# Turning listed rows: from two TensorE transpositions to one VectorE transposition of 32x32 blocks, with the rows loaded by blocks

## The chip, the cores and the metric

The kernel runs on one core of a Trainium2 chip. The metric is the device time of one execution in microseconds (us), lower is better. Three runs of the kernel before gave 1203.69, 1200.79 and 1199.48 us, median 1200.79.

The engines are TensorE (PE; PEld is its weight load), VectorE (DVE), ScalarE (ACT), GpSimd (POOL) and SyncE (SP), which issues most DMAs. "SPq" in a row is SyncE's own instruction queue.

## The reference

Two layers, each a residual block: x = x + ffn(cond(x)). x holds 64 samples of 64 channels by 1024 elements, so 4096 rows of 1024, float32.

```python
# layer 0
c0 = grouped_conv1d(x, L0_cond_weight, taps=9, groups=4) + (cond_128 @ L0_cond_c_weight.T)[:, :, None] + bias
base = c0 @ base_w.T + base_b
hidden = c0 @ A.T                              # 64 ranks
w, e = top2(softmax(c0 @ router_w.T))          # 2 of 16 experts, weights divided by their sum
x = x + base + 0.5 * sum_k(w_k * hidden @ B[e_k].T)
# layer 1
att = softmax(mlp(cond_128))                   # 8 mixtures
c1 = (sum_m att_m * weight_m) @ x + sum_m att_m * bias_m     # a 64x64 mixing of the channels, per sample
g = top2 of 28 gates (c1 @ gate_W.T), softmax over the two
x = x + c1 @ base_W.T + lora_up(2 * g * (c1 @ lora_A.T))     # 28 experts of rank 8
```

The change is in `w_k * hidden @ B[e_k].T` of layer 0: each row goes through two of sixteen matrices of 64 by 1024.

## The kernel before

**Tiles.** The 4096 rows are 32 tiles of 128. `step0` handles a tile of layer 0, `step1` one of layer 1; every engine has its own program with functions of these names, and they meet at semaphores. In a step TensorE multiplies the turned tile (`yh`, `yl`, high and low part) by the weights in three banks: `z[2]` holds the small columns (with the 64 ranks and the gates), `z[0]` and `z[1]` the rest. All products are made of three float32r matmuls (high x high, low x high, high x low), as `three` writes them.

**Lists.** Rather than multiplying each row by all sixteen `B`, the kernel sorts. In `step0` VectorE scales the row's 64 ranks by its two weights (`listed`), and GpSimd scatters the two copies (`scatter`) into `hs_dram`, where every expert has a list of its own. When a wave of 16 tiles is through, TensorE multiplies the lists by the experts' matrices, a listed tile of 128 rows at a time. Four listed tiles (`PER`) make a listed step, twelve listed steps (`WS`) a wave. Wave 0 is worked off beside the tiles 18 to 29 of layer 0, wave 1 beside the tiles 2 to 13 of layer 1. The products go to `zs_dram`, and GpSimd adds them to the rows with gathering DMAs in layer 1.

**A listed step before the change.** SyncE loads four tiles of 128 rows by 64 ranks (`load_ht`), each as 128 rows of 256 B, two side by side in one buffer `ht[j]` of 128x128; a register read from the table `tab_row` says which tile. It also loads the experts' matrices `bd` (`load_bd`, which waits until TensorE is done with the last ones) and stores the products (`store_zs`). TensorE turns the two buffers with two transpositions into the PSUM bank `prep` (`turn_ht`, line 1508), so that ranks lie on the partitions: two experts' 64 ranks in 128. ScalarE copies the bank as the high part `hh` (`ht_high`), VectorE subtracts it for the low part `hl` (`ht_low`), and one step later TensorE multiplies: `listed_pair(s, 0)` after the small bank, `listed_pair(s, 1)` after `z[0]` in layer 0 and after `z[1]` in layer 1. ScalarE copies the products out (`outputs`, tiles `zt`).

**Where the turning stands.** TensorE has it in `step0` behind `rank` and ahead of the conv of the tile after next (line 1670), and in `step1` ahead of the last matmuls `over_h` (line 1747). VectorE has `ht_low` at the end of `step0`, behind `rank0`, and in `step1` ahead of the two adds that empty `z[0]` and `z[1]` (line 1433). SyncE has the loads for listed step s + 1 at the start of `listed_step`, ahead of the `bd` loads. The order on each engine is that of the written code; there is no scheduler.

**SyncE and the output adds.** In `step1` SyncE loads the rows of the tile after next but one (`load_xr`) and starts `listed_step` only when VectorE has emptied both banks of the tile before.

## Time and profile before

| | |
|---|---|
| median of 3 runs | 1200.79 us |
| the profiled execution, its own time | 1200.46 us |
| its span | 1198.5 us |
| PE busy | 1171.6 us, 98% |
| ACT busy | 767.6 us, 64% |
| DVE busy | 706.4 us, 59% |
| POOL busy | 297.5 us, 25% |
| DMA | 267.15 MB, mean 223 GB/s |
| mean granted TensorE clock | 0.998 |

The profile is of one execution. Times count from the start of the span. A busy time is that in which at least one instruction of the engine ran; idle time of an engine that isn't the bottleneck costs nothing. The lists of wave 0 are worked off from about 302 to 530 us, those of wave 1 from about 600 to 868 us.

### The profile page before, as it was taken

How to read it: one execution, taken by the hardware profiler on the slowest of the kernel's cores; microseconds unless marked ns; L12 is line 12 of the kernel's file. 1: busy time of each engine (PE TensorE's matmuls, PEld its weight loads, DVE VectorE, ACT ScalarE, POOL GpSimd, SP SyncE). 2: the span in 40 equal slices, each digit the busy share in tenths (PEclk: the TensorE clock that was granted, in tenths of full speed). 3: DMA queues.
4: the chain of work that ended last, by engine and by line, in shares of the span. 5: the costliest groups of instructions: out<-in, count | busy, mean ns of one | idle time of the engine just before them, and what ended most of it. 6: DMA issues, size and time to landing. Idle time of an engine off the chain costs nothing.

```text
span 1198.5 us, 22055 instructions
## 1 busy us (share of the span) xinstructions
PE 1171.6 (98%) x6783; PEld 1034.3 (86%) x6783; DVE 706.4 (59%) x1985; ACT 767.6 (64%) x1746; POOL 297.5 (25%) x315
## 2 busy tenths in 40 slices
PE   6999999999999999999999999999999999999998
PEld 6999999999899999898787787787788888888887
DVE  6677778777465655557764444454445555555552
ACT  5566667666586776864667767767645665755751
POOL 4111733323222223234312112111131222222200
PEclk9999999999999999999999999999999999999999
DMA  9566566775999999979699999999875455455410
GB/s 333 185 241 258 191 225 229 285 268 165 253 319 327 311 322 311 325 269 242 127 245 304 268 293 311 281 292 299 269 165 118 99 123 110 118 123 118 110 53 36
DMA packets 84698, 267.15 MB, mean 223 GB/s; under 512 B 23248, under 2 KB 27472, under 8 KB 77360
## 3 DMA queue, kind: packets, MB, share of 16 engines
q1 hardware_dynamic: 72608, 230.12, 58.4%
q0 software_dynamic: 11600, 36.06, 17.0%
q8 instruction: 24, 0.39, 0.1%
q10 hardware_dynamic: 432, 0.30, 0.1%
q14 instruction: 34, 0.28, 0.1%
HBM read 154.24 MB, written 112.20 MB: 222 GB/s over the span
## 4 chain that ended last, share of the span: by engine, by line
PE 41%; DMA 7%; SPq 1%; issue 1%; DVE 1%; ACT 1%; POOL 0%; ACTq 0%; POOLq 0%; DVEq 0%
PE z L1461 12%; PE z L1462 12%; PE z L1463 12%; DMA ht<-hs_dram 3%; DMA xin<-zs_dram,gpos 2%; DMA xin<-x_dram 1%; PE c L1461 1%; PE c L1463 1%; PE c L1462 1%; PE c L1528 1%; PE prep L1725 1%; DMA x<-zs_dram,gpos 1%; DVE xb L1433 1%; PE c L1532 1%; PE c L1530 1%
## 5 line engine op out<-in xcount | busy, mean ns | idle before, releaser
L754 ACT ACTIVATE moved<-mid 32x256 f32<-32x256 f32 x944 | 392.2, 415 | 139.0 <-DVE mid L1023 114.6
L1461 PE MATMUL z<-w_1h,yh 128*128 128x384 f32 (+1 forms) x512 | 190.0, 371 | 0.0
L1461 PE MATMUL z<-w_0h,yh 128*128 128x384 f32 (+1 forms) x512 | 187.4, 366 | 0.2 <-DVE xb L1433 0.2
L1463 PE MATMUL z<-w_1l,yh 128*128 128x384 f32 (+1 forms) x512 | 185.8, 363 | 0.0
L1463 PE MATMUL z<-w_0l,yh 128*128 128x384 f32 (+1 forms) x512 | 185.8, 363 | 0.0
L1462 PE MATMUL z<-w_1h,yl 128*128 128x512 f32 (+1 forms) x504 | 183.0, 363 | 0.0
L1462 PE MATMUL z<-w_0h,yl 128*128 128x512 f32 (+1 forms) x504 | 182.8, 363 | 0.0
L669 POOL TENSOR_TENSOR carrier<-ones_col 128x1 f32<-128x1 f32 x96 | 25.5, 266 | 539.1 <-DVE den L1117 131.8
L1461 PE MATMUL z<-w_2h,yh 128*128 128x336 f32 (+1 forms) x512 | 152.9, 299 | 2.1 <-DVE yl L1031 2.1
L1463 PE MATMUL z<-w_2l,yh 128*128 128x336 f32 (+1 forms) x512 | 152.5, 298 | 0.0
L1462 PE MATMUL z<-w_2h,yl 128*128 128x252 f32 (+1 forms) x504 | 149.9, 297 | 0.0
L661 POOL TENSOR_TENSOR xb<-xin,bias0b 128x1024 f32<-128x1024 f32 x32 | 78.3, 2447 | 246.0 <-DMA x_dram<-xb 232.5
L812 ACT ACTIVATE e<-top,negm 128x2 f32<-128x2 f32 x64 | 18.4, 287 | 169.4 <-DVE negm L1058 169.4
L1044 DVE STREAM_TRANSPOSE mid<-moved 128x512 f32<-128x512 f32 x58 | 37.9, 691 | 134.2 <-ACT moved L754 134.2
L1461 PEld LDWEIGHTS z<-w_0h,yh 128*128 128x128 f32 x512 | 96.1, 188 | 15.0 <-issue 4.4
L1031 DVE TENSOR_TENSOR yl<-mid,yh 128x512 fp32r<-128x512 f32 x116 | 74.8, 685 | 57.8 <-PE z L1463 57.8
L1461 PEld LDWEIGHTS z<-w_1h,yh 128*128 128x128 f32 x512 | 96.2, 188 | 13.6 <-issue 4.4
L1463 PEld LDWEIGHTS z<-w_1l,yh 128*128 128x128 f32 x512 | 96.1, 188 | 10.4
L1463 PEld LDWEIGHTS z<-w_0l,yh 128*128 128x128 f32 x512 | 96.1, 188 | 10.2
L1462 PEld LDWEIGHTS z<-w_0h,yl 128*128 128x128 f32 x504 | 94.6, 188 | 10.2
L1462 PEld LDWEIGHTS z<-w_1h,yl 128*128 128x128 f32 x504 | 94.7, 188 | 9.2
L1461 PEld LDWEIGHTS z<-w_2h,yh 128*128 128x128 f32 x512 | 96.5, 188 | 4.0 <-issue 2.6
(217 smaller groups left out, 2587.8 us busy)
## 6 DMA issues: line engine op xcount, KB each, us to landing
bd<-bd_dram SPq DMA_DIRECT2D x96, 512.0 KB, 9.0
zs_dram<-zt SPq DMA_DIRECT2D x96, 512.0 KB, 10.2
hs_dram<-zt SPq DMA_DIRECT2D x34, 512.0 KB, 6.6
x8raw<-in_x_dram SPq DMA_DIRECT2D x32, 516.0 KB, 4.4
xin<-in_x_dram SPq DMA_DIRECT2D x32, 512.0 KB, 6.9
x_dram<-xb SPq DMA_DIRECT2D x32, 512.0 KB, 5.2
out_dram<-xb SPq DMA_DIRECT2D x32, 512.0 KB, 4.7
bd_dram<-bd SPq DMA_DIRECT2D x8, 1024.0 KB, 6.5
```

The costliest lines, as they stand in the source:

```text
L661: nc.gpsimd.tensor_tensor(xb[u][:, :], xin[u][:, :], bias0b[:, :], ALU.add).then_inc(xb_ready, 1)
L669: nc.gpsimd.tensor_tensor(carrier[:, :], ones_col[:, :], ones_col[:, :], ALU.add).then_inc(carried, 1)
L754: return nc.scalar.activation(o, i_, ACT.Copy)
L812: nc.scalar.activation(e12[:, :], top8[:, 0:2], ACT.Exp, bias=negm[:, :], accum_out=e12sum[:, :]).then_inc(s.exp, 1)
L1031: V.tensor_tensor(o, v, turned_rows(s, t, yh[u], b)[0], ALU.subtract).then_inc(s.y_lo[b], 1)
L1044: mm = V.transpose(mid[:, :].rearrange("p (k q r) -> p q k r", k=KC, r=Q)[:, :, k, :], moved[:, :].rearrange("p (q k c) -> p q k c", k=KC, ...
L1433: V.tensor_tensor(xb[u][:, w], z[b][:, 0:w.stop - w.start], x1[v][:, w], ALU.add)\
L1461: T.matmul(o, ah, wh, start=start, stop=False, **kw)
L1462: T.matmul(o, al, wh, start=False, stop=False, **kw)
L1463: return T.matmul(o, ah, wl, start=False, stop=stop, **kw)
L1528: T.matmul(o[half][:, :], hh[ranks(v), j, :], bd[j][ranks(v), 0, w], start=True, stop=False)
L1530: T.matmul(o[half][:, :], hl[ranks(v), j, :], bd[j][ranks(v), 0, w], start=False, stop=False)
```

## The change

Where a buffer `ht[j]` held 128 rows by 128 columns, the new `ht` holds 32x32 blocks. SyncE loads each listed tile in two DMAs instead of one, one for each half of its 64 columns. A DMA fills 32 partitions: the 128 rows are four blocks of 32, which lie side by side, and each run is 32 columns, 128 B. A block so lies in the quadrant (the group of 32 partitions) in which its columns have to stand after turning. One VectorE transposition, which turns every 32x32 block in its place, then makes the whole `ht_turned` for the four tiles. TensorE's `turn_ht` goes; ScalarE and VectorE read `ht_turned` instead of the bank. The semaphore `ht_ps` becomes `ht_done`, raised by VectorE; SyncE waits for it before it reloads `ht`. The four waits for the loads (`ht_in`) stand on VectorE now.

```diff
--- before.py
+++ after.py
@@ -172,7 +172,8 @@
         braw = [sb(over, f"braw{w}", [2 * R0, L]) for w in range(2)]
         over.close()
         bd.append(sb(ctx, "bd1", [2 * R0, 2, L], F32R))
-        ht = [sb(ctx, f"ht{j}", [P, 2 * R0]) for j in range(PER // 2)]
+        ht = sb(ctx, "ht", [P, PER // 2, P // Q, Q])
+        ht_turned = sb(ctx, "ht_turned", [2 * R0, PER // 2, P])
         hh = sb(ctx, "hh", [2 * R0, PER // 2, P], F32R)
         hl = sb(ctx, "hl", [2 * R0, PER // 2, P], F32R)
         mbrow = sb(ctx, "mbrow", [P, 1])
@@ -331,8 +332,8 @@
         ht_in = [sem(f"ht_in{v}") for v in range(4)]
         bd_in = [sem(f"bd_in{v}") for v in range(4)]
         zs_out = [sem(f"zs_out{v}") for v in range(4)]
-        ht_ps, hh_ready, hl_ready, zt_ps, zt_out = (
-            sem(n) for n in ("ht_ps", "hh_ready", "hl_ready", "zt_ps", "zt_out"))
+        ht_done, hh_ready, hl_ready, zt_ps, zt_out = (
+            sem(n) for n in ("ht_done", "hh_ready", "hl_ready", "zt_ps", "zt_out"))
         x1_hi, x1_lo = sem("x1_hi"), sem("x1_lo")
         mbrow_ready = sem("mbrow_ready")
         mprod_done, msum_done, mix_hi, mix_lo, mix_zero = (sem(n) for n in ("mprod_done", "msum_done", "mix_hi", "mix_lo", "mix_zero"))
@@ -343,7 +344,7 @@
 
         x_t = x.rearrange("s c l -> (s c) l").rearrange("(t p) l -> t p l", p=P)
         out_t = out.rearrange("s c l -> (s c) l").rearrange("(t p) l -> t p l", p=P)
-        hs_t = [a.rearrange("(t p) c -> t p c", p=P) for a in hs_dram]
+        hs_q = [a.rearrange("(t q p) c -> t p q c", p=Q, q=P // Q) for a in hs_dram]
         zs_t = [a.rearrange("(t p) c -> t p c", p=P) for a in zs_dram]
         x1_t = x1_dram.rearrange("(t p) l -> t p l", p=P)
         hs_parts = [a.rearrange("(p j r) c -> j p (r c)", p=P, c=R0, r=L // R0) for a in hs_dram]
@@ -443,10 +444,12 @@
 
             def load_ht(s, w, first=False):
                 if not first:
-                    sp.wait_ge(ht_ps, s)
+                    sp.wait_ge(ht_done, s)
                 for v in range(PER):
                     at = sp.value_load(tab_row[0:1, PER * s + v, :], min_val=0, max_val=E0 * CAP // P - 1)
-                    sp.dma_start(ht[v // 2][:, ranks(v)], hs_t[w][at]).then_inc(ht_in[v], 16)
+                    for i in range(R0 // Q):
+                        p = R0 * (v % 2) + Q * i
+                        sp.dma_start(ht[p:p + Q, v // 2, :, :], hs_q[w][at, :, :, Q * i:Q * (i + 1)]).then_inc(ht_in[v], 16)
 
             def load_bd(s, v, first=False):
                 e = sp.value_load(tab_expert[0:1, PER * s + v, :], min_val=0, max_val=E0 - 1)
@@ -825,11 +828,11 @@
 
             def ht_high(s, first=False):
 
-                act.wait_ge(ht_ps, s + 1)
+                act.wait_ge(ht_done, s + 1)
                 if not first:
                     act.wait_ge(zt_ps, PER * s)
                     act.wait_ge(hl_ready, s)
-                copy(hh[:, :, :].rearrange("p j r -> p (j r)"), prepp[:, 0:PER // 2 * P]).then_inc(hh_ready, 1)
+                copy(hh[:, :, :], ht_turned[:, :, :]).then_inc(hh_ready, 1)
 
             def outputs(s, v, banks, first=False):
 
@@ -1209,10 +1212,14 @@
                 mix_sum(t)
                 mix_low(t)
 
+            def ht_turn(s):
+                for v in range(PER):
+                    dve.wait_ge(ht_in[v], 16 * R0 // Q * (s + 1))
+                V.transpose(ht_turned[:, :, :].rearrange("p j (q r) -> p j q r", r=Q), ht[:, :, :, :]).then_inc(ht_done, 1)
+
             def ht_low(s):
                 dve.wait_ge(hh_ready, s + 1)
-                V.tensor_tensor(hl[:, :, :].rearrange("p j r -> p (j r)"), prepp[:, 0:PER // 2 * P],
-                                hh[:, :, :].rearrange("p j r -> p (j r)"), ALU.subtract).then_inc(hl_ready, 1)
+                V.tensor_tensor(hl[:, :, :], ht_turned[:, :, :], hh[:, :, :], ALU.subtract).then_inc(hl_ready, 1)
 
             step = [0]
 
@@ -1315,6 +1322,8 @@
                 residual(i, u, 1)
                 if tables:
                     tiles_of_lists(0)
+                if turn is not None:
+                    ht_turn(turn)
                 rank0(t, u, w)
                 if turn is not None:
                     ht_low(turn)
@@ -1422,6 +1431,7 @@
                 if at(t, 0):
                     tiles_of_lists(1)
                 if turn is not None:
+                    ht_turn(turn)
                     ht_low(turn)
 
                 dve.wait_ge(x1_stored[u], 16 * (TILES // 2))
@@ -1504,18 +1514,6 @@
                         mm = T.transpose(tp[n][:, P * g:P * (g + 1)], mid[:, NB * (GROUPS * n + g):NB * (GROUPS * n + g + 1)],
                                          ident[:, :])
                     mm.then_inc(a0.y_ps[n], 1)
-
-            def turn_ht(s, first=False):
-
-                for v in range(PER):
-                    pe.wait_ge(ht_in[v], 16 * s + 16)
-                if first:
-                    pe.wait_ge(tab_ready, 2)
-                else:
-                    pe.wait_ge(hl_ready, s)
-                for j in range(PER // 2):
-                    mm = T.transpose(prepp[:, P * j:P * (j + 1)], ht[j][:, :], ident[:, :])
-                mm.then_inc(ht_ps, 1)
 
             def listed_pair(s, j):
 
@@ -1666,8 +1664,6 @@
                     if first:
                         turn_conv(1)
                     rank(t, w)
-                if turn is not None:
-                    turn_ht(turn, first=at(turn, 0))
                 if exists(t + 2):
                     if lists:
                         pe.wait_ge(zt_out, PER * s + 3)
@@ -1743,8 +1739,6 @@
                 pe.wait_ge(a1.hT_lo, t + 1)
                 if first:
                     first_tiles(1)
-                if turn is not None:
-                    turn_ht(turn)
                 if first:
                     pe.wait_ge(lb_lo, 2)
                 for b in range(2):
```

TensorE in a step of layer 0 in wave 0, before (`z` and `c` are banks, `prep` the turned rows, `small_upper` and `small_ones` belong to the ranking):

```order
L1599 MATMUL z<-onehot,small_upper 128x32 [waits l0_z_out2,listed_ready]
L1600 MATMUL z<-before,small_ones 128x32
L1517 MATMUL prep<-ident,ht 128x128 [waits ht_in3,ht_in2,hl_ready,ht_in1,ht_in0]
L1517 MATMUL prep<-ident,ht 128x128
L1461 MATMUL c<-x8h,th 128x256 [waits x8_lo,l0_c_out0,x8_hi,zt_out]
```

and the same place now:

```order
L1473 MATMUL z<-w_1l,yh 128x384
L1597 MATMUL z<-onehot,small_upper 128x32 [waits l0_z_out2,listed_ready]
L1598 MATMUL z<-before,small_ones 128x32
L1471 MATMUL c<-x8h,th 128x256 [waits x8_lo,l0_c_out0,x8_hi,zt_out]
L1472 MATMUL c<-x8h,tl 128x256
```

The conv follows the ranking at once, and no instruction of TensorE waits for `ht_in`.

VectorE at the end of the same step now (`yl` is the low part of the next tile, `xb` the residual rows, `mid` the conv's output):

```order
L1034 TENSOR_TENSOR yl<-mid,yh 128x512 [waits l0_y_hi1]
L1282 TENSOR_TENSOR xb<-z,xb 128x384 [waits base_done1]
L1218 STREAM_TRANSPOSE ht_turned<-ht 128x256 [waits ht_in2,ht_in3,ht_in1,ht_in0]
L1113 TENSOR_REDUCE rank<-comb 128x2 [waits before_ready]
L1114 TENSOR_SCALAR placef<-idxf 128x2
L1116 TENSOR_TENSOR placef<-placef,rank 128x2 [waits before_ready]
L1118 CAST place_of<-placef 128x2 [waits before_ready]
L1120 COPY den<-placef 128x1
L1222 TENSOR_TENSOR hl<-ht_turned,hh 128x256 [waits hh_ready]
L1026 TENSOR_TENSOR mid<-c,cbT 128x2x2x128 [waits l0_c_ps0]
```

Before, the transposition was not there and `hl` read `prep`; the rest stood in the same order. The ranks, `hl` and the conv's output now stand behind the wait for the four loads.

SyncE's loads of one listed tile, before:

```order
L448 TENSOR_LOAD tab_row
L448 ISA x2
L449 ISA
L449 DMA ht<-hs_dram 128x64
L448 ISA
```

and now:

```order
L449 TENSOR_LOAD tab_row
L449 ISA x2
L452 ISA
L452 DMA ht<-hs_dram 32x4x32
L452 ISA
L452 DMA ht<-hs_dram 32x4x32
L449 ISA
```

One DMA and one register instruction are added for each tile, four of each in a listed step; the table is read as often as before.

## Rows read from the trace of the kernel before

**Rows 1.** The page, busy time, share of the span and instructions.
```profile
PE 1171.6 (98%) x6783; PEld 1034.3 (86%) x6783; DVE 706.4 (59%) x1985; ACT 767.6 (64%) x1746; POOL 297.5 (25%) x315
```

**Rows 2.** By stretch: busy times, then PEclk, DMA share, GB/s.
```profile
330.00:492.00 162.00, 162.00 (x1061) 147.45 (x1058) 97.80 (x294) 120.31 (x280) 40.00 (x33) 1.00 1.02 317
622.00:860.00 238.00, 235.43 (x1275) 188.40 (x1272) 111.92 (x295) 167.03 (x379) 44.88 (x52) 1.00 1.03 292
299.00:302.00 3.00, 0.11 (x3) 0.02 (x2) 2.49 (x10) 0.00 (x0) 0.19 (x1) 1.00 0.13 29
302.00:305.00 3.00, 2.98 (x16) 3.00 (x17) 0.57 (x2) 0.38 (x1) 1.96 (x2) 0.59 0.81 201
305.00:308.00 3.00, 3.00 (x21) 3.00 (x20) 1.23 (x2) 0.40 (x1) 0.00 (x0) 0.84 1.06 247
```

**Rows 3.** TensorE's waits: us in total, times, longest.
```profile
PE prep L1517 <- DMA ht<-hs_dram: 5.5, 5, 2.9
```

**Rows 4.** Timeline of TensorE, wave 0, with and without a turning: start, us.
```profile
341.18 0.18 PE L1600 MATMUL z<-before,small_ones 128*128 128x32 bf16 x1
...
341.37 0.36 PE L1461 MATMUL c<-x8h,th 128*128 128x256 f32 x1
...
529.82 0.18 PE L1600 MATMUL z<-before,small_ones 128*128 128x32 bf16 x1
529.85 0.36 PE L1461 MATMUL c<-x8h,th 128*128 128x256 f32 x1
```

**Rows 5.** The same in wave 1, with and without a turning.
```profile
621.86 0.39 PE L1532 MATMUL t<-bd,hh 64*128 64x512 f32 x1
...
622.37 0.48 PE L1461 MATMUL z<-lbh,h1h 112*128 112x512 f32 x1
...
864.86 0.39 PE L1532 MATMUL t<-bd,hh 64*128 64x512 f32 x1
865.18 0.50 PE L1461 MATMUL z<-lbh,h1h 112*128 112x512 f32 x1
```

**Rows 6.** Wave 0's start: SyncE's and TensorE's timeline; `bd` loads of 300:307.
```profile
296.81 3.63 SPq L449 DMA_DIRECT2D ht<-hs_dram  x4
301.20 4.76 SPq L455 DMA_DIRECT2D bd<-bd_dram  x4
...
310.43 0.49 PE L1528 MATMUL c<-bd,hh 64*128 64x512 f32 x1
...
L455 SPq DMA_DIRECT2D bd<-bd_dram x4: 487/504/553, 301.2 to 305.5; - x4
...
DMA to landing us min/median/max: 5.0/6.3/7.8
```

**Rows 7.** A step of wave 0: `ht` loads of 346:359, VectorE's timeline.
```profile
L449 SPq DMA_DIRECT2D ht<-hs_dram x4: 332/333/337, 346.7 to 350.3; - x4
...
DMA to landing us min/median/max: 7.6/8.9/10.2
...
361.70 0.55 DVE L1275 TENSOR_TENSOR xb<-z,xb 128x384 f32<-128x384 f32 x1
```

**Rows 8.** A late step of wave 1: `ht` loads of 672:688, VectorE's timeline.
```profile
L449 SPq DMA_DIRECT2D ht<-hs_dram x4: 337/338/363, 672.6 to 676.4; - x4
...
DMA to landing us min/median/max: 12.9/14.3/15.8
...
692.81 0.69 DVE L1433 TENSOR_TENSOR xb<-z,xin 128x512 f32<-128x512 f32 x1 [0.61 <-PE z L1463]
```

**Rows 9.** SyncE's waits from 322 to 492 us.
```profile
SPq L421 <- PE c L1463: 21.2, 9, 2.8
```

**Rows 10.** Durations min/median/max of DVE's transpositions; a wait; `hh`, `hl`.
```profile
L1040 DVE STREAM_TRANSPOSE mid<-moved x36: 400/402/446, 336.5 to 488.6; 128x256 f32<-128x256 f32 x36
...
DVE comb L1102 <- PE z L1600: 8.5, 9, 2.1
...
690.31 0.42 ACT L754 ACTIVATE hh<-prep 128x256 fp32r<-128x256 f32 x1
690.76 0.42 DVE L1214 TENSOR_TENSOR hl<-prep,hh 128x256 fp32r<-128x256 f32 x1 [1.07 <-ACT hh L754]
```

## The prediction

> **What bounds the kernel now.** I read the page first, for the engine that has no idle time. TensorE is busy for 1171.6 of 1198.5 us, all others for under two thirds of the span [rows 1]. So a microsecond counts if TensorE spends it or waits for it. Next, the rows by stretch: in the two stretches that work on lists (330 to 492 us and 622 to 860 us) TensorE is busy for 162.00 of 162.00 and 235.43 of 238.00 us, and the DMA share there is 1.02 and 1.03 [rows 2]. The reader should keep both: TensorE sets the pace there, and the DMA engines have nothing to spare that this view could show. Then TensorE's waits: for `ht`, the tile that the change touches, it waits 5 times, 5.5 us in all, the longest 2.9 us [rows 3]. That longest is the first step of wave 0, the other four are in wave 1 and sum to 2.6 us. Right behind the first one the granted clock is 0.59 for 3 us and 0.84 for the next 3 [rows 2]; at half speed part of that time, TensorE loses 3 x 0.41 + 3 x 0.16 = 1.7 us more than the wait itself.
>
> **What goes from TensorE.** 24 steps turn a listed group with two transpositions each. A single one is 272 to 331 ns long in the trace, but they overlap their neighbours, so what counts is start to start. In wave 0 the conv matmul starts 341.37 - 341.18 = 0.19 us after the ranking matmul where the pair stands between them, and 529.85 - 529.82 = 0.03 us where it doesn't [rows 4]: 0.16 us, twelve times, 1.9 us. In wave 1 it is 622.37 - 621.86 = 0.51 against 865.18 - 864.86 = 0.32 [rows 5]: 0.19 us, twelve times, 2.3 us. Together 4.2 us. The Trainium skill, VectorE: DVE Perf Modes, "The three transpose paths", lists 390 ns for a TensorE transposition of 128x128 and advises TensorE for it if PSUM will do as destination; at that price 48 of them would be 18.7 us, but the trace shows a quarter of it, because the pair is hidden in the pipeline, so by these rows the rule's advice costs little and its removal brings little.
>
> The four short waits of wave 1 go as well: 2.6 us [rows 3]. Nothing behind the missing transposition on TensorE needs `ht` directly; it needs `hl`, in its next step. What takes its place on VectorE is judged below.
>
> **The first step of wave 0.** Here the removed wait uncovers another. SyncE issues four `ht` loads from 296.81 to 300.44, and then four `bd` loads from 301.20 to 305.96 [rows 6]. A pair of `bd` halves is needed by the first listed pair on TensorE, which now starts at 310.43 [rows 6]. The second `bd` load is issued about 1.4 us after the first, at 302.6, and lands some 6 us later (the four take 5.0 to 7.8 [rows 6]), near 308.6. Without the 2.9 us wait, the 1.7 us of slow clock and the pair itself TensorE would be there at 305.6 and stand until `bd` lands. And `bd` lands later than before, because four more `ht` DMAs are issued ahead of it.
>
> What does one more DMA cost on SyncE? One that takes no new table entry: the instruction is 0.333 us [rows 7], with some register work around it; the full pitch of today's with the entry read from the table is (3.63 - 0.33) / 3 = 1.10 us [rows 6]. The bounds per step are 4 x 0.33 = 1.3 and 4 x 1.10 = 4.4 us. I take 0.5 each, 2.0 us, nearer to the bare instruction since the entry isn't read again. A DMA with more dimensions may be dearer: `bd`'s instruction is 0.504 us [rows 6]; with that for all eight it is 2.0 + 8 x 0.17 = 3.4 us.
>
> So `bd` lands near 310.6, TensorE stands for 5 us in place of 2.9, and goes on 0.2 us later than before. The clock then probably falls again as it did after the 2.9 us, which costs up to 1.7 us, of which I take 1.3. The term is a loss of 1.5 us. Its ends: if the landing did not move, a gain of 1.9 us; at 4.4 us for the issues a loss of 2.6 + 1.7 = 4.3 us.
>
> **What comes onto VectorE.** One transposition of 128x256 per step: the same form takes 0.402 us in the trace [rows 10]. In wave 0 it waits for `ht` after the third residual add, ahead of the ranks. In the step shown the last load is issued at 350.3 and lands 7.6 us later, at 357.9; VectorE ends that add at 361.70 + 0.55 = 362.25 [rows 7]. So 2 us of later landing fit, with 2.4 to spare. Behind it are queued the ranks (their scatter is GpSimd's, which idles), `hl`, and the conv output of the next tile, on which ScalarE's moves and the next transposition hang. That ring has some air: VectorE idles 8.5 us in 9 steps for the ranking matmul alone [rows 10], 0.9 us a step, against 0.4 added. ScalarE takes `hh` from SBUF instead of PSUM while it would wait for the conv output. Cost nothing; if the cover is gone, 0.4 us x 11 = 4 us.
>
> In wave 1 it stands before `hl` and the two output adds. Where `ht` is early, VectorE reaches it while ScalarE still copies `zt`, and `hh` starts no later than now. In a late step, one of the four waits, the last load is issued at 676.4 and lands 12.9 us later, at 689.3, and the last add ends at 692.81 + 0.69 = 693.5 [rows 8]. 2 us later is 691.3; then 0.40 for the transposition, 0.42 each for `hh` and `hl` [rows 10], 2 x 0.65 for the adds and 0.3 of hand-overs give 694.1, 0.6 us after today's end. TensorE asks for the first of these banks only after the 24 matmuls of the small bank and six of mixing of its next step, so it doesn't stand. But SyncE issues the next loads behind these adds, and the late steps are those with the slowest loads (12.9 us after the last issue against 7.6 above). I give back 0.5 us for it. If the ring closed, each step would cost its 0.6 us: 12 x 0.6 = 7 us is the far end.
>
> **SyncE and the DMA engines.** In wave 0 SyncE waits 21.2 us in 9 steps for the end of the conv [rows 9], 2.4 us a step, and some 0.8 us elsewhere: 2.0 us fit, 3.4 us wouldn't quite. In wave 1 it waits for the listed pairs right after the `ht` loads. The DMA engines get 1024 packets of 128 B per step for 512 of 256 B. Between 299 and 302 us nearly nothing but such `ht` packets moved: a share of 0.13 at 29 GB/s [rows 2], so 0.13 x 16 x 3000 = 6240 ns for 87 KB, or 340 packets, 18 ns each. One of half the bytes costs between half and all of that, so a step gets between 0 and 512 x 18 / 16 ns = 0.6 us longer on every DMA engine, out of 18.9 us. Cost nothing while TensorE is the bound.
> The Trainium skill, DMA: Bandwidth & Descriptors, speaks against the change here ("How a descriptor splits into AXI transactions", and the overhead per packet in the section before it): a transfer that does not start on a 256 B boundary is fetched from the boundary below, so the upper half of each row would cost as much as the whole row; with its fixed 3 cycles a row goes from 11 to 18 cycles, an estimate of 0.4 us more per step. No row of this trace has such packets.
>
> **Sum.** 4.2 + 2.6 - 1.5 - 0.5 = 4.8 us less. The profiled execution took 1200.46 us (1198.5 of it the span), so 1195.7; it lay 0.33 us below the median of the runs, so 1196.0 us.
>
> **Rivals.**
> 1. No change: the gains in wave 1 are given back, because the loads of the next tiles and their two gathered adds, which hang on the output adds, become the ring that sets the pace, and SyncE's extra work eats its slack. The four waits then return at another place: 1196.0 + 2.6 + 2 = 1200.6 us. For it: the DMA share and the late steps. Against it: `ht` lands before it is asked for in 7 of the 11 later steps.
> 2. Slower: SyncE becomes the bound in wave 0. It decides from 3.2 us more per step. At 4.4 us the step grows by 1.2 us, eleven times, 13 us, the first step loses 4.3 and wave 1 keeps its 4.9: 1200.8 + 13 + 4 - 5 = 1213 us; at 3.4 us it is about 1202. Against it: the table entry isn't read again, and it is the larger part of the pitch.
> 3. Slower: the DMA engines are the bound already and TensorE only looks full because both fit. For it: share 1.02 and 1.03 [rows 2]. Then nothing is gained in the list stages, every step costs 0.3 to 0.6 us more, 23 x 0.3 = 7 us at the least, and the first step 1.5: 1209 us or more. Against it: TensorE would then stand somewhere in 330 to 492 us, and it doesn't. With the 0.4 us of the Trainium skill's rule above it would be 1212 us.
> 4. Better than forecast: `bd` lands as early as now and the clock doesn't fall: 1196.0 - 3.4 = 1192.6 us.
>
> **Chances.** Forecast (1193.5 to 1198.5) 0.37; rival 4 0.10; rival 1 0.27; rival 2 0.13, nearly half of it with the small price; rival 3 0.13. The likeliest is the forecast, 1196.0 us. The range is 1190 to 1208: it leaves out the dear form of rival 2 and most of rival 3. About 0.3%, 3.6 us, is what a measurement of this kernel can tell from no change. Faster by more than that (below 1197.2): most of the forecast, rival 4 and a little of rival 1, 0.46. Slower by more (above 1204.4): rival 3, the dear half of rival 2 and a little of the rest, 0.24. Within it 0.30.
>
> **What would show it.** Right: no wait of TensorE for `ht` and none for `hl`; start to start 0.03 and 0.32 us at the two places; a wait of 4 to 5 us before the first listed pair, for `bd`, with a clock below 1 behind it; the `ht` group on SyncE 5 to 6 us long instead of 3.6 to 4.1; VectorE's 24 transpositions near 0.40 us. Wrong: TensorE waits in the steady steps of wave 0 (for `yl` or `x8l`: rivals 2 or 3), SyncE without any wait for the conv, an `ht` group over 7 us, or landing times of `bd` that grow with the steps.

## The result, and the profile after

| | before | after |
|---|---|---|
| median | 1202.17 us, 4 runs (1199.48 to 1203.69) | 1215.45 us, 4 runs (1212.16 to 1216.74) |
| the profiled execution, its own time | 1200.46 us | 1214.24 us |
| its span | 1198.5 us | 1212.5 us |
| mean granted TensorE clock | 0.998 | 0.996 |

The ratio is 1.0098, 95% interval [1.0070, 1.0127]. The changed kernel is slower by 1%; forecast were 0.4% faster and a range that ends at 1208 us. A few executions took far longer than all others of their kernel (4051 us for one of e5, 1279 and 4067 us for two of the kernel before), and every ratio and interval here leaves them out.

First the stretches of the changed kernel. The columns are those of [rows 2]: busy times of PE, PEld, DVE, ACT, POOL, then PEclk, DMA share, GB/s.

```profile
303.00:306.00 3.00, 3.00 (x20) 2.77 (x18) 1.76 (x8) 0.42 (x1) 0.55 (x2) 1.00 0.37 104
306.00:309.00 3.00, 0.06 (x1) 0.00 (x0) 1.40 (x8) 2.11 (x6) 1.71 (x2) 1.00 1.06 227
309.00:312.00 3.00, 0.72 (x4) 0.69 (x6) 0.95 (x6) 1.88 (x7) 0.00 (x0) 0.78 1.01 225
312.00:315.00 3.00, 3.00 (x15) 2.15 (x12) 0.77 (x5) 0.79 (x2) 0.00 (x0) 0.50 1.00 223
330.00:492.00 162.00, 158.75 (x1031) 144.37 (x1029) 94.48 (x302) 116.67 (x274) 43.83 (x34) 1.00 1.00 308
622.00:860.00 238.00, 231.78 (x1225) 183.36 (x1224) 112.86 (x291) 160.42 (x359) 40.31 (x52) 0.99 1.01 282
```

TensorE stands for some 5 us at the start of wave 0, with the slow clock behind it (0.50 is the lower of its two levels, 1.2 GHz). In both list stretches it now has holes, 3.25 and 6.22 us against 0 and 2.57 before. The DMA engines are as full as before but move less: 308 GB/s for 317, and 282 for 292.

TensorE's waits in the list stages, 299 to 868 us, of the changed kernel (us in total, times, longest), which answer to [rows 3]:

```profile
PE c L1526 <- DMA bd<-bd_dram: 5.2, 1, 5.2
PE c L1471 <- DVE mixl L1209: 5.0, 4, 3.3
PE z L1471 <- DVE xb L1443: 3.2, 5, 1.6
PE c L1471 <- ACT zt L757: 2.6, 4, 0.7
PE c L1471 <- DVE x8l L1017: 1.9, 2, 1.1
```

The wait for `ht` is gone from TensorE. The first row is the wait for `bd` that took its place. The other four, 12.7 us, were 0.4 us before: for the mixing of wave 1 (`mixl`), for emptied banks (`xb`, `zt`), and for the input of the conv (`x8l`).

The wait for `ht` has not gone from the kernel. It stands on VectorE now, in wave 1 ahead of the output adds, 7.6 of the 10.5 us there; in e1 below, with the old loads, it is 1.7 us.

```profile
DVE ht_turned L1218 <- DMA ht<-hs_dram: 10.5, 5, 3.8
```

Then SyncE's waits in the two list stages. The first block is the changed kernel from 322 to 492 us, for [rows 9]; the second the kernel before from 622 to 860 us; the third the changed kernel there.

```profile
SPq L422 <- PE c L1473: 1.6, 1, 1.6
```
```profile
SPq L455 <- PE t L1532: 66.2, 21, 3.9
SPq L459 <- ACT zt L754: 13.9, 7, 11.3
SPq L597 <- DVE xb L1433: 11.3, 11, 1.9
```
```profile
SPq L600 <- DVE xb L1443: 16.3, 9, 2.8
SPq L462 <- ACT zt L757: 14.6, 11, 6.4
SPq L458 <- PE t L1530: 11.1, 6, 3.7
```

A wait of SyncE is its slack: it stands until the rest of the kernel has caught up. In wave 0 this fell from 21.2 to 1.6 us, in wave 1 from 91.4 to 42.0. SyncE is late now, and what it issues late lands late.

What took the slack? SyncE's timeline of one step of wave 0 in the changed kernel (the `ht` loads as a group), and one of wave 1; start, us:

```profile
350.64 5.86 SPq L452 DMA_DIRECT2D ht<-hs_dram  x8
...
702.67 8.56 SPq L452 DMA_DIRECT2D ht<-hs_dram  x8
```

Then all instructions of the tile `ht` on SyncE, and VectorE's transpositions (ns min/median/max):

```profile
L452 SPq DMA_DIRECT2D ht<-hs_dram x192: 316/321/3401, 296.9 to 849.1; - x192
L1218 DVE STREAM_TRANSPOSE ht_turned<-ht x24: 428/445/447, 304.2 to 862.0; 128x256 f32<-128x256 f32 x24
```

In [rows 7] the group was 3.9 us, so the 2.0 us of the forecast is what one step shows (5.9). But in wave 1 it takes up to 9.1 us: single `ht` instructions last up to 3.4 us where the longest of before was 0.363. Over 600 ns are 27 of SyncE's DMA instructions in the two list stages (none before), 24 us above their usual length, and not only `ht`'s.

Last a place where SyncE is late with nothing to wait for: the end of its loop over wave 1 (`Fori(1, 3)`, four steps a pass), in the kernel before and in the changed one. The columns are start and us; `L598`/`L601` stores the output, `L563`/`L566` is the row load of the next pass.

```profile
737.90 0.33 SPq L598 DMA_DIRECT2D out_dram<-xb  x1
738.96 0.35 SPq L563 DMA_DIRECT2D x<-x_dram  x1
```
```profile
750.77 0.34 SPq L601 DMA_DIRECT2D out_dram<-xb  x1
757.30 0.35 SPq L566 DMA_DIRECT2D x<-x_dram  x1
```

From the one to the other are 1.06 us before and 6.53 us after. In the records of SyncE's sequencer the branch that closes the loop ends at 751.29 us, and the next instruction starts at 756.98: 5.69 us in which it waits for no semaphore. In the kernel before this is 0.22 us.

By all signs SyncE waits for its own instructions there. The profile counts the DMA packets that bring instructions (kind "instruction", 8 KB each on queue 14). These are the rows of the kernel before and of the changed one, over the whole execution:

```profile
q14 instruction: 34, 0.28, 0.1%
```
```profile
q14 instruction: 42, 0.34, 0.1%
```

In the second pass of the loop, 751.3 to 842 us, the changed kernel fetches five of them, two within the stop; the kernel before fetches none in its second pass.

What follows shows in the chain of waits of the changed kernel behind it: start, us, what; of SyncE's rows the first and last stand here.

```profile
757.30 0.35 SPq L566
...
774.68 0.33 SPq L601
775.27 13.91 DMA xin<-x_dram
790.08 11.91 DMA xin<-zs_dram,gpos
802.33 0.32 issue
802.86 9.27 DMA xin<-zs_dram,gpos
```

For a whole step, 757 to 775 us, the chain runs through SyncE alone, from one DMA instruction to the next. So two row loads go out 7.0 and 5.8 us after their banks were emptied, at 757.30 and 775.27; in the other steps it is 0.5 to 1.1 us. Behind each hang the two additions by GpSimd's gathering DMAs, and behind them ScalarE, VectorE and TensorE's mixing. This is the ring of rival 1: from the issue of the load to the last landing it takes some 37 of the 44 us that two steps last.

The stop doesn't explain all of wave 1. TensorE's longest wait there, 3.3 us for `mixl`, ends at 747.66 us, ahead of the branch. Its row load was issued on time, 0.8 us after the bank was emptied, but it and its two additions took 43 of the 44 us to land:

```profile
701.38 15.80 DMA xin<-x_dram
718.06 12.26 DMA xin<-zs_dram,gpos
731.12 13.43 DMA xin<-zs_dram,gpos
```

### The profile page after: what moved, and what is told of

Read it like the earlier page. It is cut to its first block, busy times and chain, and to the rows that moved or that the text cites. A ratio compares the mean times of both kernels' runs of the same rounds, so it can differ in the third digit from the quotient of the medians.

```text
span 1212.5 us, 22260 instructions
## 1 busy us (share of the span) xinstructions
PE 1174.3 (97%) x6735; PEld 1033.4 (85%) x6735; DVE 712.3 (59%) x2009; ACT 768.1 (63%) x1746; POOL 298.0 (25%) x315
## 4 chain that ended last, share of the span: by engine, by line
PE 28%; DMA 16%; SPq 3%; issue 2%; ACT 1%; DVE 1%; POOL 0%; POOLq 0%; ACTq 0%; DVEq 0%
PE z L1472 9%; PE z L1471 9%; PE z L1473 9%; DMA xin<-zs_dram,gpos 6%; DMA x<-zs_dram,gpos 4%; DMA xin<-x_dram 4%; DMA x<-x_dram 2%; ACT zt L757 1%; PE c L1471 1%; PE c L1473 1%; PE c L1472 1%; SPq L452 1%; DVE xb L1443 1%; SPq L455 1%; SPq L449 1%
## 5 line engine op out<-in xcount | busy, mean ns | idle before, releaser
L664 POOL TENSOR_TENSOR xb<-xin,bias0b 128x1024 f32<-128x1024 f32 x32 | 82.0, 2562 | 254.3 <-DMA x_dram<-xb 240.5
L1471 PEld LDWEIGHTS z<-w_1h,yh 128*128 128x128 f32 x512 | 96.2, 188 | 13.6 <-issue 4.4
L1472 PEld LDWEIGHTS z<-w_0h,yl 128*128 128x128 f32 x504 | 95.4, 189 | 10.1
```

The lines of the kernel that those rows point to most:

```text
L664: nc.gpsimd.tensor_tensor(xb[u][:, :], xin[u][:, :], bias0b[:, :], ALU.add).then_inc(xb_ready, 1)
L1471: T.matmul(o, ah, wh, start=start, stop=False, **kw)
L1472: T.matmul(o, al, wh, start=False, stop=False, **kw)
```

## The experiments

All are timed against the kernel before on the same chip. Theory A: SyncE's instruction stream, lengthened by four more DMAs a step, sets the pace of the list stages. Theory B: twice the packets do, on the DMA engines or by holding SyncE up. Theory C: VectorE's transposition does. Theory D came last, when the stop behind the branch was found: much of it is this stop.

**e1, the turning on VectorE, loads as before.** The changed kernel with four DMAs of 512 packets a step; the rows come whole and not by blocks, so the listed products aren't those of the reference.

```
+ sp.dma_start(ht[...][:, ranks(v)], hs_t[w][at]).then_inc(ht_in[v], 16)     # 128 rows of 256 B
```

> The turning stays on VectorE, but the rows are loaded as before the change: four DMAs of 128 rows of 256 B per listed step, so the values of the listed products are not those wanted. Three theories for the 13 us that the change lost. SyncE theory (the number of DMAs: four more issues per step fill SyncE's time): the loss goes and the forecast gains remain, 1192 to 1197 us, and SyncE again waits over 15 us for the conv between 322 and 492 us. Packet theory (1024 packets of 128 B per step instead of 512): the same, 1192 to 1197 us. VectorE theory (its wait for the loads and the later hl hold back the conv output and the output adds): the loss stays, 1208 to 1216 us.

Measured: 1197.45 us, 0.9967 [0.9933, 1.0001]. TensorE waits 3.0 us for `bd` at the first listed pair and little elsewhere; SyncE still waits 16.2 us in 9 steps for the conv. The time is 0.5 us above the range of theories A and B and far below that of C. Theory C falls: this half of the change loses nothing and perhaps gains the 4 us.

**e2, the turning on TensorE, loads as changed.** The kernel before with the changed kernel's eight DMAs; TensorE turns whole buffers, for which these blocks don't lie right, so the listed products aren't the reference's.

> The kernel before, TensorE turning, with the new loads: eight DMAs of 32 partitions, 1024 packets of 128 B per step; the values of the listed products are not those wanted. SyncE theory and packet theory: slower than before by at least the 13 us, 1213 to 1222 us, since TensorE now waits for the later loads itself. VectorE theory: within 3 us of before plus what TensorE waits at the first step (2 us), 1200 to 1206 us.

Measured: 1220.58 us, 1.0138 [1.0097, 1.0178]. TensorE waits for `ht` 14 times, 22.4 us. So the loss is in the loads.

**e3, four DMAs, 1024 packets of 128 B, 64 partitions each.** The turning on VectorE; the halves don't lie where it needs them, so the products aren't the reference's.

> VectorE turns, and each tile is loaded by one DMA (four per step, as before the change), but in 256 packets of 128 B (1024 per step, as after it); the values of the listed products are not those wanted. SyncE theory: like the run with the old loads, 1192 to 1198 us. Packet theory: like the changed kernel, 1210 to 1217 us, and DMA instructions of SyncE that last over 0.6 us. VectorE theory: 1208 to 1216 us too, without those long instructions.

Measured: 1211.53 us, 1.0085 [1.0057, 1.0113]. The number misleads: 5 us of it fall behind the lists, where the kernels don't differ. The buffer `ht` was padded, so all buffers behind it lay 32 B further, and the matmuls there were longer. The same group from 870 to 1200 us in e3 and in the kernel before (us busy, mean ns):

```profile
L1472 PE MATMUL z<-w_0l,yh 128*128 128x512 f32 x144 | 56.9, 395 | 0.0
```
```profile
L1463 PE MATMUL z<-w_0l,yh 128*128 128x512 f32 x144 | 56.2, 390 | 0.0
```

**e5, the same over 128 partitions** (two packets of 128 B a row, `ht` padded too; again not the reference's products).

> VectorE turns; four DMAs per step over 128 partitions, as before the change, but each row as two packets of 128 B (1024 per step); wrong values in the listed products. It differs from the run with the old loads (1197 us) in the number of packets alone, and unlike the one-DMA run over 64 partitions (1211.5 us) its DMA instruction should last 0.33 us when it isn't held up. Packet theory: 1205 to 1212 us, with DMA instructions over 0.6 us where 1300 and more packets are outstanding. SyncE theory: 1195 to 1200 us.

Measured: 1209.86, 1212.12 and 1222.83 us, 1.0119 [1.0066, 1.0173], with the same 5 us behind the lists and a wide interval. Both kernels are no measure of the packets alone, so that was done again.

**e9, e5 without the padding.**

```
+ o = ht[:, v // 2, :, :].rearrange("p (h k) r -> p h k r", k=2)[:, :, v % 2, :]
+ sp.dma_start(o, hs_h[w][at]).then_inc(ht_in[v], 16)        # 128 rows of 2 x 128 B
```

> As the changed kernel, but each listed tile comes in one DMA over all 128 partitions, every row as two packets of 128 B: four DMAs and 1024 packets a step. The two halves lie in two blocks that aren't neighbours, and all buffers lie where the changed kernel has them (the earlier kernels with 1024 packets in four DMAs had moved the buffers behind ht by 32 B, and their matmuls outside the list stages were 1.2% longer, some 7 us in all). The listed products are wrong. Theory A, the number of DMAs alone costs: as with four DMAs and 512 packets, 1195 to 1200 us, SyncE's waits for the conv in 322 to 492 us 14 us or more, no DMA instruction over 0.7 us. Theory B, the packets alone cost as well, since SyncE's instructions are held up while some 1400 packets and more are outstanding: 10 to 20 instructions over 0.7 us in each list stage, most of the loss in wave 1 and at the first step, 1203 to 1209 us.

Measured: 1206.14 us, 1.0025 [1.0005, 1.0046], in the range of theory B. Against e1 this is 0.6% more, give or take 0.4. An `ht` instruction takes 0.57 us for 0.33, and about 20 DMA instructions are held up over 0.7 us, most of them in wave 1. So packets seem to cost too, by these medians less than half of the way from e1 to the changed kernel; how much of it is the longer instruction and how much the packets themselves, e9 doesn't separate.

**e4, the number of DMAs.** The kernel before, its products unchanged, each listed tile in two DMAs of 64 rows (512 packets).

```
+ for i in range(2):
+     q = slice(64 * i, 64 * (i + 1))
+     sp.dma_start(ht[v // 2][q, ranks(v)], hs_t[w][at, q, :]).then_inc(ht_in[v], 16)
```

> The kernel before, TensorE turning, right values; each tile is loaded by two DMAs of 64 rows, so eight DMAs per step but still 512 packets of 256 B. SyncE theory: slower than before by 8 us or more, 1209 to 1218 us, SyncE without waits for the conv in wave 0. Packet theory and VectorE theory: within 3 us of before plus 2 us at the first step, 1200 to 1205 us.

Measured: 1234.58 us, 1.0267 [1.0224, 1.0310], the slowest of all and 16 us above even the range of theory A, which had not reckoned with a dearer instruction. An instruction that fills 64 partitions takes 0.477 us, not 0.33; the group is 7.2 to 7.8 us, SyncE's wait for the conv 0.5 us, and TensorE waits for `ht` 28.8 us in 12 times. All instructions of the tile in e4:

```profile
L451 SPq DMA_DIRECT2D ht<-hs_dram x192: 468/477/1103, 297.1 to 866.8; - x192
```

**e6, eight DMAs into 32 partitions as in the changed kernel, but 64 packets of 256 B each** (512 a step; not the reference's products).

> VectorE turns; eight DMAs per step into 32 partitions as in the changed kernel, but 64 packets of 256 B each (512 per step); wrong values in the listed products. It differs from the run with the old loads in the number of DMAs alone. SyncE theory: 1203 to 1212 us, SyncE with under 8 us of waits for the conv between 322 and 492 us, no long DMA instructions. Packet theory: 1195 to 1200 us.

Measured: 1217.88 us, 1.0132 [1.0106, 1.0158]. With no more packets than before it is at least as slow as the changed kernel, and 6 us above the range of theory A, far above that of B.

**e12, four tiny DMAs more.** The kernel before, its products unchanged; TensorE turns.

```
+ sp.dma_start(extra[32 * v:32 * v + 32, :], hs_t[w][at, 0:32, 0:8]).then_inc(ht_in[v], 16)
```

> The kernel before, right values, with four DMAs more in each listed step: behind each load of a listed tile one of 32 rows by 32 B into a buffer that nobody reads, 32 packets and 1 KB each. SyncE's instructions are as many as in the changed kernel, the bytes and packets nearly those of before (640 for 512). Theory A, the issue stream of SyncE is enough to slow the kernel: the ht group takes 5.3 to 5.9 us for 3.6, SyncE's waits for the conv in 322 to 492 us fall from 21 to under 6 us, the first wait of TensorE grows by some 2 us, 1206 to 1213 us. Theory B, only packets count: few held-up instructions, no loss but in the first step, 1202 to 1205 us.

Measured: 1220.08 us, 1.0132 [1.0105, 1.0158], above the range of theory A and far from B. Four DMAs of 1 KB a step, an instruction of 0.39 us each, cost 16 us. With hardly more packets or bytes than before, and with the stop that comes with them (6.95 us), they lose more than the whole change. The tile in e12, and TensorE's longest wait:

```profile
L451 SPq DMA_DIRECT2D extra<-hs_dram x96: 368/392/1239, 297.6 to 851.1; - x96
```
```profile
PE prep L1519 <- DMA extra<-hs_dram: 17.4, 11, 4.8
```

**e7 and e8, two issues fewer.** In the changed kernel (e7) and in the kernel before (e8) the products of two listed tiles are stored by one DMA, which waits for both; products unchanged.

```
- sp.wait_ge(zt_out, PER * s + v + 1)      # for each of four
+ sp.wait_ge(zt_out, PER * s + v + 2)      # for each of two pairs
```

> The changed kernel with right values, and the products of two listed tiles stored by one DMA instead of two, so two DMAs fewer per listed step for SyncE at the same bytes and packets. SyncE theory: some 1.2 us per step come back to SyncE, the time falls by 3 to 8 us to 1205 to 1211 us. Packet theory: no change, 1211 to 1216 us.

> The kernel before, with the same paired stores, right values. Both theories: SyncE has slack before the change, so the same time as before within 3 us, 1198 to 1204 us; if SyncE's slack is worth something even there, up to 4 us faster.

Measured: e7 1213.7 us, 1.0089 [1.0063, 1.0116], where theory A had at most 1211; e8 1204.77 us, 1.0023 [0.9996, 1.0050]. In e7 SyncE's wait for the conv is back to 10.1 us and wave 0 is 3.5 us shorter, but 33 DMA instructions over 600 ns remain and wave 1 loses as before. Less issuing at the price of a later store gains nothing that these runs resolve.

**e10 and e11, the order at the start of a wave.** The first two `bd` loads ahead of the `ht` loads, in the changed kernel (e10) and in the kernel before (e11); products unchanged.

```
+ for v in range(2):
+     load_bd(WS * w, v, first=w == 0)
  load_ht(WS * w, w, first=w == 0)
+ for v in range(2, 4):
```

> The changed kernel, right values, with the first two bd loads of each wave ahead of the ht loads instead of behind them. If TensorE's wait of 5.2 us at the first listed pair is SyncE's issue order alone, the two bd halves are issued about 5.5 us earlier and the wait falls; but the last ht load is then issued about 2.3 us later, and hh and hl hang on it: 2 to 3 us of the 5.2 remain, now for hh or hl, 1211 to 1214 us. If it is the DMA engines or the landing time that binds, the wait stays near 5 us, 1214 to 1217 us.

> The kernel before, right values, with the same order at the start of each wave: the first two bd loads ahead of the four ht loads. The turning on TensorE, which already waits 2.9 us for ht, then waits some 2.3 us more, with the slow clock behind it, and bd is there when it is asked for: 1203 to 1206 us. If the loads of the start are bound by their landing instead, the order costs nothing: 1200 to 1203 us.

Measured: e10 1210.97 us, 1.0059 [1.0038, 1.0080]: the wait at the first listed pair falls from 5.2 to 3.5 us. e11 1213.27 us, 1.0056 [1.0029, 1.0083], a miss: I expected up to 1206. TensorE waits for `ht` 6.9 us at the start of wave 0, 4.0 at that of wave 1, and 1.9 in the middle of wave 0; I had counted only the first, and 1.7 us less.

**e13, the stores issued by ScalarE.** The changed kernel, its products unchanged. The number of DMAs and packets stays, four of them leave SyncE's stream.

```
+ def store_pair(s, v, w):                      # ScalarE, behind outputs(s, v) and (s, v + 1)
+     act.wait_ge(zt_out, PER * s + v + 2)
+     for k in (v, v + 1):
+         act.dma_start(zs_t[w][PER * s - LISTED * w + k], zt[k][:, :]).then_inc(zs_out[k], 16)
```

> The changed kernel, right values, with the stores of the listed products issued by ScalarE, two behind each second pair of outputs, instead of SyncE. DMAs and packets are as many as in the changed kernel; SyncE has four fewer a step (some 0.4 us each with their register work) and no wait for zt. Theory A, SyncE's instruction stream is the bound: it gets its slack back (12 us or more of waits for the conv in 322 to 492 us), TensorE's waits in the steady steps go, 1200 to 1207 us. Theory B, more DMAs cost on the DMA side, whoever issues them: 1212 to 1218 us, loads landing as late as before. ScalarE has some 2 us a step more to do, of 5 us that it waits; if that is too much, TensorE waits for ScalarE's tiles.

Measured: 1205.22 us, 1.0029 [1.0008, 1.0050], as theory A has it. SyncE's waits in 322 to 492 us, and the stretch of wave 1:

```profile
SPq L422 <- PE c L1476: 32.8, 9, 4.8
```
```profile
622.00:860.00 238.00, 237.87 (x1272) 189.59 (x1272) 120.47 (x314) 171.63 (x384) 43.07 (x54) 1.00 1.03 299
```

TensorE is full again in wave 1, although the stop behind the branch is still there (5.80 us): a row load goes out 6.8 us late, but the row loads of wave 1 land sooner, after 9.2 and 10.0 us in the median for the two buffers (11.5 and 13.6 in the changed kernel), and the ring has air for it. Only 4 DMA instructions last over 600 ns, with the packets of the changed kernel. What stays is the first step: 5.4 us for `bd`.

The edit changes two things at once. It takes four instructions a step from SyncE, and it moves the stores to ScalarE's own DMA queue, so that SyncE's queue is shorter; the sooner landings may come from the second. No run here parts the two.

**e14, the same in the kernel before.** Products unchanged.

> The kernel before, right values, with the stores of the listed products issued by ScalarE in the same way. If SyncE had slack enough in both waves, nothing is gained: 1200 to 1205 us. If wave 1 was already paced by SyncE's loads in its late steps, the four waits for ht there (2.6 us) go: 1196 to 1200 us.

Measured: 1200.35 us, 0.9969 [0.9949, 0.9989]. This beats both kernels. In wave 1 TensorE has no wait for `ht` any more:

```profile
622.00:860.00 238.00, 238.00 (x1290) 190.32 (x1289) 115.02 (x302) 170.67 (x384) 43.05 (x53) 1.00 1.04 295
```

So SyncE's stream, or the length of its queue, made the four short waits of wave 1 in the kernel before, and relieving it takes them away without the change. Its profiled execution, 1200.25 us, isn't shorter than that of the kernel before, for a wait of 4.2 us between the waves stands in it; the 0.3% rest on the runs.

**e15, e13 with e10's order.** Products unchanged.

> The changed kernel, right values, with both: the stores issued by ScalarE, and the first two bd loads of a wave ahead of the ht loads. The start order gained 4 us with the stores on SyncE. If it and the steady loss are separate terms, this is 2 to 4 us below the kernel with the stores alone, 1197 to 1204 us under theory A; if the gain came from the same slack, it is equal to it.

Measured: 1205.97 us, 1.0031 [1.0006, 1.0056], equal to e13 and not 2 to 4 us below. What the order gained in e10 doesn't come on top of the slack.

**e16 to e18, no branch back.** SyncE's loop of wave 1 is written out, in the changed kernel (e16), in e13 (e17) and in e12 (e18); products unchanged. The DMAs, their order and their number stay.

```
- with sp.Fori(1, 3) as i:
+ for i in range(1, 3):
      for v in range(4):
          step1(i, v, lists=True)
```

> The changed kernel, right values, with SyncE's loop of wave 1 (two passes of four steps) written out, so that no branch goes back. Theory D, the stop of 5.7 us behind that branch, which delays a row load in the chain of the gathered adds, is a large part of wave 1's loss: the row load at 757 us is issued 0.8 us after the emptied bank and not 7 us, the holes of TensorE behind 800 us (some 4 us) go, 1208 to 1212 us. Theory A, the steady issue time alone: 1213 to 1217 us as now.

> The changed kernel, right values, with the stores issued by ScalarE and the same loop written out. e13 has the stop too (5.8 us) but TensorE is busy for 237.87 of 238 us in wave 1, so both theories expect little: 1203 to 1206 us, e13 being at 1205.2.

> The kernel before, right values, with the four tiny DMAs a step of e12 and the same loop written out. e12 has a stop of 7.0 us behind the branch at 749.6 us and a TensorE hole of 6.6 us in the step at 780 us. Theory D: the hole goes, 1211 to 1215 us. Theory A: 1217 to 1222 us.

Measured: e16 1207.09 us, 1.0028 [1.0004, 1.0051]; e17 1203.49 us, 1.0009 [0.9990, 1.0029]; e18 1212.32 us, 1.0083 [1.0054, 1.0113]. Theory D holds: e16 and e18 are faster than the same kernels with the loop. The changed kernel was at 1.0098, so the medians give this one stop 0.7%, but from the two intervals it can be anything from about 0.3 to 1.1%. For e12 it is 0.5%, from about 0.1 to 0.9. The trace is at the low side: the profiled execution of the changed kernel loses 4.3 us behind the stop, 0.4%. The stretch of wave 1 in e16 has 4.96 us of holes for 6.22:

```profile
622.00:860.00 238.00, 233.04 (x1247) 184.68 (x1246) 116.64 (x299) 165.37 (x370) 42.26 (x52) 1.00 1.04 290
```

Every row load is issued within 1 us of its bank being emptied. This profiled run took 1210.88 us, above the median of its kind, so its holes are rather too many. e17 can't be told from the kernel before.

## Why the prediction was wrong

In the two profiled executions the first listed pair of each step gives the balance: 3.5 us lost up to the second step of wave 0, 3.7 in the rest of wave 0, 6.9 in wave 1, 0.2 gained between; 13.9 in all, for the 13.8 us between their times. Within wave 1 the loss first shrinks by 1.7 us, then grows by 4.4 at the late landings before the stop and by 4.3 behind the stop. Forecast was a gain of 4.8.

**Right: the turning.** In the changed kernel's timeline of TensorE, for [rows 4, 5], the next matmul follows where the pair stood before:

```profile
344.64 0.18 PE L1598 MATMUL z<-before,small_ones 128*128 128x32 bf16 x1
344.66 0.36 PE L1471 MATMUL c<-x8h,th 128*128 128x256 f32 x1
...
628.77 0.39 PE L1530 MATMUL t<-bd,hh 64*128 64x512 f32 x1
...
629.10 0.50 PE L1471 MATMUL z<-lbh,h1h 112*128 112x512 f32 x1
```

0.02 and 0.33 us for the forecast 0.03 and 0.32. e1 puts this half of the change at 0.33% to the good, its interval ending at no change. VectorE's transposition, 0.445 us for the forecast 0.402, was hidden; what wasn't is the wait for `ht` ahead of it, 10.5 us in the changed kernel, where the forecast had room for later landings. The 390 ns that the prediction took from the Trainium skill, VectorE: DVE Perf Modes, "The three transpose paths", are for bf16, and these tiles are float32. No term of the sum hangs on them.

**Right in its mechanism, too small: the first step.** The wait moved to `bd` and is 5.2 us long ("TensorE stands for 5 us"). But the clock stayed at 0.50 to 0.78 for longer than behind the 2.9 us wait: 3.5 us lost, not 1.5, within its ends (1.9 gained to 4.3 lost).

**Wrong: what four more DMAs on SyncE cost.** The step was priced by its instructions: "2.0 us" a step, "2.0 us fit, 3.4 us wouldn't quite", and "0.5 us" given back in wave 1. Three things failed there.

- *The stop behind the branch was in no term.* The closing branch of the loop of wave 1 costs 5.69 us where it cost 0.22, once, and e16 puts this at 0.7% of the kernel's 1%, with an interval from 0.3 to 1.1 and 0.4 by the trace. I counted instructions by their time and not by what they do to the loop. All kernels that keep the loop and have four more loads a step show it (5.65 to 6.95 us); with the loads' number unchanged it is 0.22 to 0.25. The Trainium skill, Runtime: NRT & Kernel Launch, "Instruction fetch mechanics", says that a taken branch whose target lies outside the engine's current window of two pages, 512 instructions, has to wait for a fetch. The traces agree: in the second pass of the loop all nine kernels with the stop fetch five packets of instructions, one or two of them within the stop, and the seven without it fetch none. The length of the loop doesn't decide it, for a pass has 332 recorded instructions of SyncE in the kernel before and 325 in e13, which stops. Its place in the program does fit: counted from the start of SyncE's program, with each loop once, the loop ends at recorded instruction 973 or earlier in the seven, and at 1005 or later in the nine. This is what a border of a page near there would do; no run was made to move the loop alone.
- *The room in wave 0.* The price was right, 2.0 us a group (5.9 for 3.9). Taken off, 18 of the 21.2 us should have left 3 us; 1.6 were left, in one step of nine, and TensorE had waits. A mean slack of 2.4 us isn't 2.4 us in each step, and 12 held-up instructions in wave 0 took 7.5 us more.
- *Wave 1.* I looked at SyncE's waits in wave 0 only. The ring of rival 1 was named with its place, but at 1200.6 us, for it was priced without anything that makes a row load late or slow to land. It has next to no air: once its landings alone took 43 of 44 us, and TensorE stood before the stop had begun.

By the medians, from e1 to the changed kernel are 1.3%: the stop 0.7, the remaining issue time with the packets 0.6, each give or take 0.4. e13 shows another cure: with four issues fewer on SyncE, and the stores on another queue, the ring bears the stop, 1.0029.

**Partly wrong: "Cost nothing while TensorE is the bound"** for the packets. e9 against e1 gives 0.6%, give or take 0.4, for them, in part because a DMA instruction with 256 packets takes SyncE 0.57 us. In all packets of the list stages the mean is 18.9 ns for one of 256 B and 13.3 ns for one of 128 B, so a step has 1024 x 13.3 less 512 x 18.9 ns on 16 engines, 0.25 us more on each, within my 0 to 0.6. By that measure two halves take 1.41 times as long as a whole row. The rule that I had weighed for rival 3 (the Trainium skill, DMA: Bandwidth & Descriptors, "How a descriptor splits into AXI transactions") made it 18 for 11 cycles, 1.6 times, because the upper half would be dearer than the lower. The trace doesn't bear the rule out: 22,805 of the 24,576 packets of 128 B take 13 ns, upper halves and lower halves alike, and a whole row takes 18. So two halves are dearer than a row by what each packet costs whatever its size, not by where it starts.

**The rivals.** Rival 2 named the engine and, with 1213 us, nearly the time, but by a step of 4.4 us more in wave 0. The step has 2.0, and half of the loss is in wave 1. Rival 3 falls with e9 and with e6, which loses as much with the packets of before. Rival 4 would have needed `bd` as early as before.

What stays open: why a DMA instruction of SyncE is held up. While it is, SyncE's queue often has 1300 to 1600 packets outstanding (issued less completed; the kernel before reaches some 1190). But e13 reaches some 1500 with 4 such instructions, and e6 has 11 with about 1000 at most outstanding in wave 0, so this count alone doesn't decide it. Open too is why the row load at 701 us landed so late, and whether the change had a part in it. Nor was it tried why e7, with only two issues fewer, keeps the holes of wave 1; its branch stops for 6.78 us too.

## What to carry to other kernels

Count a DMA as work of the engine that issues it, whatever its size, and lay it beside that engine's waits in every stage, not beside their mean in one. Look too at the sequencer's records behind the closing branch of each loop: added instructions can move the loop so that its start has to be fetched again, the issuing engine then stands for some 6 us, and if a load of the slowest ring is next in its order, that comes out at the end (here some 0.4 to 0.7%, cured by writing the loop out). In the kernel before, moving four stores a step to an engine with air was worth 0.3% and beat both kernels; no form of the new layout that keeps the products did so.

## What the runs showed of the hardware

- The stop of 5.65 to 6.95 us behind a loop's closing branch on SyncE, with five packets of instructions fetched in the pass behind it, against 0.22 to 0.25 us and no such packet. The loop with 325 recorded instructions had it, one with 332 had not.
- A DMA instruction on SyncE took 0.32 us into 32 partitions (64 or 128 packets; 0.39 with 32 packets of 32 B in e12), 0.33 into 128 (128 packets), 0.57 into 128 and 0.56 into 64 with 256 packets, and 0.477 into 64 (64 packets).
- A DMA packet of 256 B took 18 ns and one of 128 B 13 ns, whether or not it started in the middle of a 256 B row.
- Moving buffers by 32 B made 512-column matmuls 395 ns long instead of 390, 5 us over the last 330 us of the kernel. Why wasn't tried; it is a trap for any experiment that pads a buffer.
- A 32x32-block transposition of 128x256 took 0.445 us in this place and 0.402 in another of the same kernel.
